# Query and key rows copied from SBUF into the score stacks, and a new order of the lead-in of a two-layer attention and mixture kernel

## The chip, the cores and the metric

One core of a Trainium2 chip runs the whole program. The metric is the device time of one execution in microseconds. TensorE is called PE below, VectorE DVE, ScalarE ACT, GpSimd POOL and SyncE SP; "SPq" and so on is an engine's sequencer, which issues DMAs.

## The reference, cut to what matters

The input is x (4 batches, 512 tokens, 256 channels) and a context of the same shape. Two layers follow each other:

```
x = x + xattn0(layernorm(x), ctx)      # 16 heads of 16 channels, biases, score bias -0.1*|i-j|
x = x + ffn0(layernorm(x))             # dense SiLU MLP + product-key retrieval: top 8 of 1024 experts, 4 heads
x = x + xattn1(layernorm(x), ctx)      # 16 heads, relu on q, k and v, no biases
x = x + ffn1(layernorm(x))             # 8 experts, top 2 by a gate, gelu MLP 256-512-256
```

Each attention is softmax(q k^T / 4 [+ bias]) v for every batch and head. What matters here is how q and k get to the place where PE multiplies them.

## The kernel before, in words

Everything is fp32, and where a product must be exact to more bits than one pass gives, a value is held as a rounded high part and the rest (low part). For attention, each head's q and k are laid in *stacks*: `sq` and `sk` hold, for each of 8 pairs of heads, 64 partitions per head of the pair (`HALF`), of which 48 (`BROW`) are three blocks of 16 rows (q: high, low, high; k: high, high, low), then 8 rows of constants (the bias by distance), then the row of maxima (`MROW`). One product over 56 or 57 partitions so gives the exact score with its bias.

A batch is prepared by *jobs*: "xt" (transposes of the normed x), "k" and "q" (projections, two of each, `i` or `s` = 0, 1 being the first or second head of each pair), "v" (values), later "on"/"wo" (output projection). For "k" and "q" ACT writes the high part into the row buffer `hl` and DVE the low part (L1593, L1594); `hl` is [128, 4, 2, 512]: index 0 and 1 are queries, 2 and 3 keys. `write_rows` (SP) then writes each to a DRAM tensor `qk_rows` by two DMAs (L468, L469), and after all eight of a batch have landed (`s_dw`), `load_stacks` and `stack` (L482) read them back in the stacks' layout, four DMAs of 192 KB for each of four head groups `g`.

An attention layer runs in steps U = -7 to 63 and a few more, 16 steps to a batch, four to a head group. Step U does the four score products for the row maxima of group (U+7)/4 (L1161; DVE reduces each, L1589; three PSUM banks), the scores by key of its own (L1175), their exponential (ACT, L905), in layer 0 a factor for near keys (POOL, L670), and the values (L1194). The table of jobs is written out by hand: `PREPARE` and `PREPARE_SECOND` (for batch 1) give the step of each job relative to its batch's step 0, `FINISH` those of the output projection, `STACKS` the steps at which SP loads the stacks, `NEXT_CTX` those of the next context. `FIRST` is the order of batch 0's jobs, ahead of the steps.

Each engine works through its own queue in order. Before the steps of layer 0: SP issues the loads of x and context of batch 0, all constants and weights, then waits for the rounded row patterns (`s_rowc`), spreads them into the stacks (`const_rows`, L493, L496: 9 or 8 partitions each), writes key rows, loads x of batches 1 to 3 and reads its half of the stacks. ACT loads wk, wq, wv, empties PSUM, writes the query rows (`first_query_rows`, L916, L917) and reads the other half (`first_stacks`, L925). DVE computes the statistics of batch 0, waits for all query weights and scales them (L1816), normalises (`first_norm`, L1667), and in its `prologue` (L1782 to L1808) turns the products of the retrieval weights (`wret`), the gate's constants and the output bias out of PSUM and computes the statistics of batches 1 to 3 at once. PE's `prologue` (L1220 to L1235) computes these products. POOL adds the output bias to x (`add_bo`) and norms the later batches (`norm`, L620); in the steps of layer 0 it also splits layer 1's expert weights into high and low parts by way of DRAM (`split_high`, `split_low`, `split_out` L655, `load_raw` L660, L661).

Layer 1's first rows are prepared at the end of ffn0; `first_rows` (SP) writes and reads them.

## Time and profile before

| | us |
|---|---|
| median of 3 runs | 1217.73 (1215.11 to 1217.9) |
| profiled execution | 1213.62 |
| its span | 1211.8 |
| PE busy | 1055.4 (87%) |
| DVE busy | 788.4 (65%) |
| ACT busy | 638.7 (53%) |
| POOL busy | 474.4 (39%) |

In the profile's rows, `L1161` is a line of the kernel, `out<-in` names the tensors, `xN` counts instructions merged into a row, and what stands in brackets with `<-` is the idle time before an instruction and what ended it. Rows of the timeline begin with start and duration in us. A DMA-issuing row (SPq, ACTq, POOL DMA_DIRECT2D) is the time that the sequencer takes to issue, not the transfer.

### The profile page before, as it was taken

To read this page: it belongs to the slowest core of one execution; us is meant where nothing else is said; L and a number is where in the kernel's file an instruction comes from. 1 tells how busy PE (TensorE), PEld (TensorE's weight loads), DVE (VectorE), ACT (ScalarE), POOL (GpSimd) and SP (SyncE) were. 2 spreads that over 40 slices of the span, in tenths; PEclk is the share of its full clock that TensorE was granted. 3 is DMA by queue.
4 is the path that set the end of the run, shared out by engine and by line. 5 is a ranking of instruction groups with operands and counts; after the bars stand their busy time and mean duration, and the time that the engine had idled before them with its cause. 6 is when DMAs were issued, how large, how long until landed. Compare 5 with 4: busy or idle time off the path is not lost.

```text
span 1211.8 us, 16920 instructions
## 1 busy us (share of the span) xinstructions
PE 1055.4 (87%) x5478; PEld 658.8 (54%) x5478; DVE 788.4 (65%) x1986; ACT 638.7 (53%) x848; POOL 474.4 (39%) x494
## 2 busy tenths in 40 slices
PE   9499899989776999999999778999999888799991
PEld 5134343434355787787777554433334334588881
DVE  3667677786489777877787334777777955244443
ACT  2146565566528667667677422565545661355550
POOL 1347777686413243343443321212323334222220
PEclk9579999999879999999999986999998998899996
DMA  7946778666999300000002330455453328222226
GB/s 186 249 148 192 228 198 264 174 206 224 255 238 233 78 1 1 1 1 1 1 1 64 103 78 1 148 165 146 117 167 93 102 63 325 66 74 71 72 62 209
DMA packets 75595, 151.71 MB, mean 125 GB/s; under 512 B 8234, under 2 KB 45356, under 8 KB 73974
## 3 DMA queue, kind: packets, MB, share of 16 engines
q1 hardware_dynamic: 62518, 99.46, 31.9%
q0 software_dynamic: 10544, 47.23, 11.2%
q10 hardware_dynamic: 2448, 3.94, 1.2%
q8 instruction: 47, 0.77, 0.3%
q14 instruction: 38, 0.31, 0.1%
HBM read 73.88 MB, written 76.25 MB: 124 GB/s over the span
## 4 chain that ended last, share of the span: by engine, by line
PE 55%; DVE 24%; ACT 8%; issue 6%; POOL 3%; DMA 3%; SPq 1%; ACTq 0%; DVEq 0%; POOLq 0%
PE ps L1296 14%; DVE negmax L1589 9%; PE ps L1194 7%; PE ps L1161 6%; PE ps L1140 4%; PE ps L1175 4%; PE ps L1149 4%; PE ps L1398 3%; PE ps L1375 3%; PE ps L1361 2%; PE ps L1203 1%; PE ps L1516 1%; DVE moe_w L1885 1%; DVE hl L1594 1%; DVE on L1609 1%
## 5 line engine op out<-in xcount | busy, mean ns | idle before, releaser
L1589 DVE TENSOR_REDUCE negmax<-ps 128x1 f32<-128x512 f32 x512 | 320.9, 682 | 68.9 <-PE ps L1161 67.2
L905 ACT ACTIVATE pt<-ps 128x1024 f32<-128x1024 f32 x256 | 256.4, 1026 | 129.9 <-PE ps L1175 129.1
L1161 PE MATMUL ps<-sk,sq 56*128 56x512 f32 x512 | 166.5, 460 | 48.0 <-DVE negmax L1589 24.7
L1194 PE MATMUL ps<-pt,v_aug 128*32 128x512 f32 x1024 | 142.6, 620 | 1.2 <-POOL pt L670 0.8
L1161 PEld LDWEIGHTS ps<-sk,sq 56*128 56x128 f32 x512 | 75.7, 200 | 105.3 <-DVE negmax L1589 76.3
L1175 PE MATMUL ps<-sq,sk 57*128 57x512 f32 x512 | 127.1, 489 | 2.5 <-DVE negmax L1589 1.4
L670 POOL TENSOR_TENSOR pt<-pt,near 128x256 f32<-128x256 f32 x128 | 92.3, 728 | 76.0 <-ACT pt L905 75.7
L1175 PEld LDWEIGHTS ps<-sq,sk 57*128 57x128 f32 x512 | 50.1, 190 | 101.2 <-issue 72.4
L835 POOL DMA_INDIRECT expert_out<-yo,dest x39 | 38.2, 980 | 116.2 <-ACT yo L1080 104.5
L751 POOL TENSOR_TENSOR w_first<-w_first,moe_w 128x1024 f32<-128x1024 f32 x16 | 38.1, 2379 | 105.7 <-DVE pt L1877 105.0
L1361 PE MATMUL ps<-sel,hl 128*128 128x512 f32 x256 | 71.7, 412 | 5.6 <-DVE pt L1877 5.6
L1296 PE MATMUL ps<-wexp,ghl 128*128 x468 | 65.9, 290 | 1.6 <-DVE ghl L1985 1.5
L1296 PE MATMUL ps<-wexp,xhl 128*128 x234 | 65.0, 414 | 1.2 <-DVE xhl L1981 1.2
L1985 DVE TENSOR_TENSOR ghl<-ps,ghl 128x512 fp32r<-128x512 f32 x39 | 26.9, 691 | 59.8 <-ACT ghl L1073 59.8
L1375 PE MATMUL ps<-wup_e,xn 128*128 128x256 f32 x256 | 62.1, 379 | 0.0
L1296 PEld LDWEIGHTS ps<-wexp,ghl 128*128 128x128 f32 x468 | 57.9, 188 | 6.4 <-issue 2.2
L806 POOL TENSOR_TENSOR x_tok<-x_tok,on 128x256 f32<-128x256 f32 x16 | 11.6, 725 | 121.7 <-DVE on L1609 121.7
L1877 DVE SCALAR_TENSOR_TENSOR moe_w<-ps,thr,moe_w 128x1024 f32<-128x1024 f32 x26 | 33.3, 1280 | 39.7 <-ACT moe_w L966 39.6
L1361 PEld LDWEIGHTS ps<-sel,hl 128*128 128x128 f32 x256 | 48.0, 188 | 16.3 <-DVE pt L1877 6.9
L966 ACT ACTIVATE moe_w<-ps,negm 128x1024 f32<-128x1024 f32 x26 | 28.9, 1112 | 52.2 <-PE ps L1361 30.3
L1375 PEld LDWEIGHTS ps<-wup_e,xn 128*128 128x128 f32 x256 | 48.1, 190 | 7.8 <-issue 1.0
L797 POOL DMA_INDIRECT expert_rows<-pay,rowi x32 | 31.8, 994 | 44.1 <-DVEq L1751 35.9
(284 smaller groups left out, 2008.2 us busy)
## 6 DMA issues: line engine op xcount, KB each, us to landing
expert_rows<-zero SPq DMA_DIRECT2D x3, 5586.0 KB, 58.0
expert_weights_split<-wst POOLq DMA_DIRECT2D x8, 2048.0 KB, 9.4
qk_rows<-hl SPq DMA_DIRECT2D x30, 512.0 KB
sq<-qk_rows SPq DMA_DIRECT2D x60, 192.0 KB, 4.6
sk<-qk_rows SPq DMA_DIRECT2D x60, 192.0 KB, 5.1
moe_w<-in_w POOLq DMA_DIRECT2D x16, 512.0 KB, 7.1
wexp<-expert_weights_split POOLq DMA_DIRECT2D x16, 512.0 KB, 4.6
wexp<-expert_weights_split SPq DMA_DIRECT2D x4, 2048.0 KB, 17.1
```

Of the source, the lines that this page charges most:

```text
L670: pool.tensor_tensor(probs, probs, near[:].unsqueeze(1).broadcast_to([P, 2, P]), ALU.mult).then_inc(s_near, 1)
L835: pool.indirect_dma_start(yg, bass.IndirectOffsetOnAxis(ap=dest[:, j:j + 1], axis=0), yo[:, j % 3, :], None, bounds_check=2 * NTOK - 1, oo ...
L905: act.activation(pt[:, 4 * (U % 2) + 2 * half:4 * (U % 2) + 2 * half + 2, :], ps[:, 2 + 2 * half:4 + 2 * half, :], ACT.Exp, scale=(BIAS, S ...
L1140: ins = pe.matmul(dst, w[L][:, part, i * P:(i + 1) * P], src[:, part, :], start=(part == 0), stop=(part == 1))
L1149: ins = pe.matmul(dst[:, part * D:(part + 1) * D], src[:, k, t * P:(t + 1) * P], w[:, k, :], start=(k == 0), stop=(k == KC - 1))
L1161: pe.matmul(ps[:, jbank(job), :], sq[r, pair, t * P:(t + 1) * P], sk[r, pair, :], start=True, stop=True).then_inc(s_job, 1)
L1175: ins = pe.matmul(ps[:, 2 + 2 * half + s, :], sk[r, pair, c * P:(c + 1) * P], sq[r, pair, :], start=True, stop=True)
L1194: ins = pe.matmul(ps[32 * j:32 * j + 32, OBANK, :], v_aug[:, b % 2, c, HG * g + j, :], pt[:, 4 * (U % 2) + j, :], start=(c == 0), stop=(c ...
L1296: ins = pe.matmul(dst, lhs(i), rhs(j), start=(first and i == j == 0), stop=(last and i == 1))
L1361: ins = pe.matmul(dst[:, j, :], turned[n % 2][:, i, h * P:(h + 1) * P], sel[:, NX * YK * j:NX * YK * (j + 1)], start=(i == 0), stop=(i == 1))
L1375: ins = pe.matmul(ps[:, YBANK, (n % 2) * D:(n % 2 + 1) * D], accT[:, c * P:(c + 1) * P], wup_e[:, c, :], start=False, stop=True, skip_grou ...
L1589: dve.tensor_reduce(negmax[:, n % 2, col:col + 1], src, AX, ALU.max, negate=True).then_inc(s_jd, 1)
```

## The change

The DRAM tensor `qk_rows`, `write_rows` and `s_dw` go. The order of the projections' columns is changed (last lines of the diff), so that the rows of one head group are 32 neighbouring partitions of `hl`; `stack` copies them straight into the stacks, three DMAs of 64 KB for each half and each of `sq` and `sk`, twelve for a group, 48 for a batch. ACT's write of the next batch's rows into `hl` now waits for the last group's copies (`s_ld[3]`). `PREPARE`, `STACKS`, `NEXT_CTX` and `FINISH` get new steps. In `first_rows` the two halves are copied one after the other.

In the lead-in SP loads x and context of batches 0 and 1, copies the key stacks, then the selector and the rest. POOL issues `const_rows` of layer 0 and the eight loads of weights. DVE rounds the row patterns and norms batch 0 before it waits for the query weights; its `prologue` goes: POOL scales the gate's columns (`gate_columns`), ACT copies the products out of PSUM, POOL takes the low parts (`wret_low`) and adds the bias (`bias_out`); the statistics of batches 1, 2, 3 go to DVE's steps -3, 0, 1, and the inverse deviations of 2 and 3 are computed by Newton steps on POOL. PE's `prologue` keeps the retrieval products; those of gate and bias follow step -4 (`gate_prologue`). ACT issues group 0's query copies ahead of emptying the value jobs, the others behind. The diff, cut:

```diff
-PREPARE = {-22: ("xt", 0), -21: ("xt", 1), -20: ("k", 0), -17: ("k", 1), -16: ("q", 0), -15: ("q", 1), -13: ("v", 0), -12: ("v", 1)}
-PREPARE_SECOND = {-17: ("xt", 0), -16: ("xt", 1), -15: ("k", 0), -14: ("k", 1), -13: ("q", 0), -12: ("q", 1), -11: ("v", 0), -10: ("v", 1)}
-FINISH = {21: ("on", 0), 22: ("on", 1), 23: ("wo", 0), 24: ("wo", 1)}
+PREPARE = {-17: ("xt", 0), -16: ("xt", 1), -14: ("k", 0), -13: ("k", 1), -12: ("q", 0), -11: ("q", 1), -10: ("v", 0), -9: ("v", 1)}
+PREPARE_1 = {-16: ("k", 0), -15: ("k", 1), -14: ("xt", 0), -13: ("xt", 1), -12: ("q", 0), -11: ("q", 1), -10: ("v", 0), -9: ("v", 1)}
+prepared = lambda L, b: PREPARE_1 if L == 0 and b == 1 else PREPARE
+STACKS = {-10: 0, -8: 1, -4: 2, 0: 3}
+FINISH = {22: ("on", 0), 23: ("on", 1), 24: ("wo", 0), 25: ("wo", 1)}
...
-STEPS = (range(-LEAD, LASTU + 9), range(-LEAD, LASTU + 18))
-prepared = lambda b: PREPARE_SECOND if b == 1 else PREPARE
-STACKS = (None, 10, 12, 12)
-NEXT_CTX = (-LEAD, -9)
+STEPS = (range(-LEAD, LASTU + 10), range(-LEAD, LASTU + 18))
+NEXT_CTX = (2, -8)
...
-        rows = nc.dram_tensor("qk_rows", (2, B, 4, 3, P, T), F32, kind="Internal").ap()
...
+            def stack(g, s, dst):
+                for i, part in enumerate((0, 1, 0) if dst is sq else (0, 0, 1)):
+                    at_row = HALF * s + DH * i
+                    sp.dma_start(dst[at_row:at_row + DH, 2 * g:2 * g + 2, :].bitcast(F32),
+                                 hl[2 * DH * g:2 * DH * (g + 1), s if dst is sq else 2 + s, part].bitcast(F32)).then_inc(s_ld[g], 16)
...
+                sp.wait_ge(s_st, 2 * (LASTU * L + NU * (b - 1) + 4 * g + 3) + 2)
                 for s in range(2):
-                    stack(L, b, g, s, sq)
-                    stack(L, b, g, s, sk)
-            def stack(L, b, g, s, dst):
-                src = rows[L, b, s if dst is sq else 2 + s].rearrange("l (i e) t -> (l i) e t", e=NPAIR)
-                sp.dma_start(dst[HALF * s:HALF * s + BROW, 2 * g:2 * g + 2, :].bitcast(F32), src[:, 2 * g:2 * g + 2, :]).then_inc(s_ld[g], 16)
+                    if g == 0:
+                        sp.wait_ge(s_jd, at[L, "k", b, s].done)
+                    stack(g, s, sk)
+                for s in range(2):
+                    if g == 0:
+                        sp.wait_ge(s_jd, at[L, "q", b, s].done)
+                    stack(g, s, sq)
...
                 sp.wait_ge(s_hd, NTL)
                 for s in range(2):
-                    const_rows(1, s, sk)
-                for g in range(NG):
-                    for s in range(2):
-                        stack(1, 0, g, s, sk)
+                    const_rows(sp, 1, s, sk)
                 for s in range(2):
-                    write_rows(1, 0, "q", s)
+                    sp.wait_ge(s_pre, 1 + s)
+                    for g in range(NG):
+                        stack(g, s, sk)
                 sp.wait_ge(s_f, NTL)
                 sp.wait_ge(s_zr, 1)
                 for s in range(2):
-                    const_rows(1, s, sq)
-                sp.wait_ge(s_dw, 128 * (B + 1))
-                for g in range(NG):
-                    for s in range(2):
-                        stack(1, 0, g, s, sq)
+                    const_rows(sp, 1, s, sq)
+                for s in range(2):
+                    sp.wait_ge(s_pre, 3 + s)
+                    for g in range(NG):
+                        stack(g, s, sq)
...
+            sp.dma_start(st_rows, a["c_rows"]).then_inc(s_rows_in, 16)
+            sp.wait_ge(s_wk, 16 * 2)
+            sp.dma_start(x_tok[:, 1], tokens(a["x"][1])).then_inc(s_x[1], 16)
+            load_ctx(0, 1)
+            for g in range(NG):
+                for s in range(2):
+                    if g == 0:
+                        sp.wait_ge(s_jd, at[0, "k", 0, s].done)
+                    stack(g, s, sk)
+            sp.dma_start(st_sel, a["c_sel"]).then_inc(s_selin, 16)
+            for b in range(2, B):
+                sp.dma_start(x_tok[:, b], tokens(a["x"][b])).then_inc(s_x[b], 16)
             for dst, src in ((tab[:], a["c_tab"]), (before16[:], a["c_before"])):
                 sp.dma_start(dst, src).then_inc(s_tab, 16)
-            sp.wait_ge(s_rowc, 1)
...
+            pool.wait_ge(s_rowc, 1)
+            for s in range(2):
+                const_rows(pool, 0, s, sk)
+                const_rows(pool, 0, s, sq)
+            for dst, src in (
+                (st_wq, a["w_ret"].rearrange("(a n) d -> n a d", n=RD)), (st_keys, a["keys"].rearrange("n h p k -> n (h p k)")),
+                (bo_bc[:], a["bo"].rearrange("(a n) -> a n", a=1).broadcast_to([P, D])), (bvc[:], a["bv"]),
+                (gw[:, :, 0:ME], kcut(a["gate"])), (gcol[:, 0:KC], a["gamma"]),
+                (gcol[:, KC:2 * KC], a["beta"]), (wo[:], kcut(a["wo0"])),
+            ):
+                pool.dma_start(dst, src).then_inc(s_w, 16)
+            own = Own(pool, s_pown)
...
+            def wret_low(k):
+                pool.wait_ge(s_wret, 2 * k + 2)
+                pool.tensor_tensor(wret[:, 1, k, :], wret_full[:, k, :], wret[:, 0, k, :].bitcast(F32), ALU.subtract).then_inc(s_wrl, 1)
+            def bias_out():
+                pool.wait_ge(s_wret, 2 * KC + 3)
+                pool.tensor_tensor(bo_bc[:], bo_full, bo_bc[:], ALU.add).then_inc(s_bo_bc, 1)
...
-                if U in (2, 3):
-                    norm(0, 2, range(2 * U - 4, 2 * U - 2))
-                if U == 4:
-                    add_bo(2)
-                if U in (14, 21):
-                    norm(0, 3, range(0, 2) if U == 14 else range(2, 4))
-                if U == 26:
-                    add_bo(3)
+                if U == 2:
+                    add_bo(0)
+                if U in (3, 4):
+                    rstd_newton(range(0, 2) if U == 3 else range(2, NEWTON))
+                if U in (4, 8):
+                    wret_low((U - 4) // 4)
+                if U in (9, 14):
+                    norm(0, 2, range(0, 2) if U == 9 else range(2, 4))
+                if U in (21, 26):
+                    norm(0, 3, range(0, 2) if U == 21 else range(2, 4))
+                if U == 33:
+                    add_bo(1)
+                if U in (45, 46):
+                    add_bo(U - 43)
...
-                        act.wait_ge(s_dw, 128 * (B * L + job.b))
+                        act.wait_ge(s_ld[NG - 1], 192 * (B * L + job.b))
...
+                    if job.kind == "v" and job.i == 0:
+                        first_stacks(0)
...
-                    for s in range(2):
-                        first_query_rows(s)
-                    for g in range(NG):
+                    for g in range(1, NG):
                         first_stacks(g)
+                    for k in range(KC):
+                        act.wait_ge(s_wret_ps, k + 1)
+                        act.copy(wret[:, 0, k, :], ps[:, 2 + k, :]).then_inc(s_wret, 1)
+                        act.copy(wret_full[:, k, :], ps[:, 2 + k, :]).then_inc(s_wret, 1)
+                    act.wait_ge(s_wret_ps, KC + 1)
+                    act.copy(bo_full, ps[:, OBANK, 0:D]).then_inc(s_wret, 1)
+                    for i in range(2):
+                        act.copy(gbc[:, i, :], ps[:, 4 + i, 0:ME]).then_inc(s_wret, 1)
+                    sqrt(1, sd[:, 1, :], mv[:, 1, :, 1])
+                    act.wait_ge(s_selin, 16)
+                    act.copy(sel[:], st_sel).then_inc(s_sel, 1)
+                    act.wait_ge(s_ci, 16 * NCI)
                     act.activation(near[:], st_dist, ACT.Exp, scale=-BIAS).then_inc(s_nr, 1)
-                    sqrt(1, sd[:, 1:B, :], mv[:, 1:B, :, 1])
                 for U in STEPS[L]:
                     Ug = LASTU * L + U
...
+                for s in range(2):
+                    if g == 0:
+                        act.wait_ge(s_jd, at[0, "q", 0, s].done)
+                    for i, part in enumerate((0, 1, 0)):
+                        at_row = HALF * s + DH * i
+                        act.dma_start(sq[at_row:at_row + DH, 2 * g:2 * g + 2, :].bitcast(F32), hl[2 * DH * g:2 * DH * (g + 1), s, part].bitcast(F32)).then_inc(s_ld[g], 16)
...
-                    pe.wait_ge(s_ld[v // 4], 64 * (B * L + job.b + 1))
+                    pe.wait_ge(s_ld[v // 4], 192 * (B * L + job.b + 1))
...
+                    if L == 0 and U == 0:
...
+                    if L == 0 and U == -4:
+                        gate_prologue()
...
+                    if L == 0 and U == -3:
+                        batch_stats(1)
+                        dve.sem_inc(s_lnv, 1)
+                    if L == 0 and U == -2:
+                        dve.wait_ge(s_lnd, 2)
+                        dve.reciprocal(rstd[:, 1, :], sd[:, 1, :]).then_inc(s_rstd, 1)
+                    if L == 0 and U in (0, 1):
+                        batch_stats(2 + U)
+                    if L == 0 and U == 2:
+                        flat_bt = lambda v: v.rearrange("p b t -> p (b t)")
+                        root_seed(flat_bt(rstd[:, 2:B, :]), flat_bt(mv[:, 2:B, :, 1]), root[:, 0, 0:2 * TT]).then_inc(s_lns, 1)
...
-            dve.wait_ge(s_wqk, 16 * 3)
-            dve.tensor_scalar(wq[0][:], wq[0][:], SCALE * UNITS, None, ALU.mult).then_inc(s_conv, 1)
+            dve.wait_ge(s_rows_in, 16)
+            dve.tensor_copy(rowc[:], st_rows).then_inc(s_rowc, 1)
             dve.wait_ge(s_lnd, 1)
             dve.reciprocal(rstd[:, 0, :], sd[:, 0, :]).then_inc(s_rstd, 1)
             first_norm()
+            dve.wait_ge(s_wqk, 16 * 3)
+            dve.tensor_scalar(wq[0][:], wq[0][:], SCALE * UNITS, None, ALU.mult).then_inc(s_conv, 1)
             dve.tensor_scalar(bqk[:, 0, :], bqk[:, 0, :], SCALE * UNITS, None, ALU.mult).then_inc(s_conv, 1)
-            dve.wait_ge(s_ci, 16 * NCI)
-            dve.tensor_copy(rowc[:], st_rows).then_inc(s_rowc, 1)
             attention(0)
...
-    order = np.array([(2 * e + s) * DH + ch for s in range(2) for ch in range(DH) for e in range(NPAIR)])
+    order = np.array([(2 * e + s) * DH + ch for s in range(2) for g in range(NG) for ch in range(DH) for e in (2 * g, 2 * g + 1)])
...
```

## Rows read from the trace of the kernel before

**Rows 1.** The page: busy us, share and instructions of each engine

```profile
PE 1055.4 (87%) x5478; PEld 658.8 (54%) x5478; DVE 788.4 (65%) x1986; ACT 638.7 (53%) x848; POOL 474.4 (39%) x494
```

**Rows 2.** The chain of waits, 0 to 130 us: start, duration, what

```profile
3.40 7.67 DMA w_first<-in_wv
...
30.56 16.81 issue
...
48.19 11.45 DVE negmax L1589 x19
...
70.34 3.72 PE ps L1140 x4
...
82.14 2.00 PE ps L1140 x4
```

**Rows 3.** The timeline of the lead-in and first steps: start, duration, engine, line, operation

```profile
11.64 1.38 DVE L1667 TENSOR_SCALAR xn<-x_tok,mv,rstd 128x256 f32<-128x256 f32 x4
...
22.08 0.75 DVE L1594 SCALAR_TENSOR_TENSOR hl<-ps,bqk,hl 128x512 fp32r<-128x512 f32 x1 [1.37 <-ACT hl L871]
...
24.64 3.78 PE L1225 MATMUL ps<-moe_w 64*128 64x64 f32 x32
...
29.26 1.30 PE L1234 MATMUL ps<-w_first,pt 128*128 128x256 f32 x4
...
39.36 1.41 DVE L1554 BATCH_NORM_STATS2 st<-x_tok 128x6 f32<-128x256 f32 x4
...
41.26 0.45 ACTq L925 DMA_DIRECT2D sk<-qk_rows  x1
...
47.38 1.19 PE L1161 MATMUL ps<-sk,sq 56*128 56x512 f32 x3 [16.81 <-issue]
...
64.81 0.65 PE L1175 MATMUL ps<-sq,sk 57*128 57x512 f32 x2
...
71.11 0.82 POOL L661 DMA_DIRECT2D moe_w<-in_w  x1
```

**Rows 4.** Windows: us, busy time by engine, PE's clock, DMA share, GB/s

```profile
core 0: us, PE busy (x) PEld busy (x) DVE busy (x) ACT busy (x) POOL busy (x), PEclk, DMA share, GB/s
14.00:22.00 8.00, 6.74 (x17) 3.44 (x18) 1.75 (x3) 2.00 (x4) 0.00 (x0) 0.79 0.44 58
28.00:38.00 10.00, 2.56 (x16) 1.85 (x15) 3.04 (x8) 0.00 (x0) 2.33 (x1) 0.60 1.04 353
...
697.00:699.00 2.00, 0.27 (x2) 0.00 (x0) 0.00 (x0) 2.00 (x3) 2.00 (x2) 1.00 0.46 49
704.00:708.00 4.00, 3.11 (x15) 2.11 (x13) 1.48 (x3) 0.11 (x1) 2.15 (x1) 1.00 1.03 214
```

**Rows 5.** The line L482 (stack DMAs), 160 to 215 us: time to landing

```profile
DMA to landing us min/median/max: 3.3/4.8/6.2
```

**Rows 6.** The timeline of layer 0's steps, several engines

```profile
98.74 0.42 SPq L482 DMA_DIRECT2D sk<-qk_rows  x1
...
123.89 0.50 PE L1161 MATMUL ps<-sk,sq 56*128 56x512 f32 x2 [2.06 <-DMA sk<-qk_rows]
...
131.41 2.43 POOL L620 TENSOR_SCALAR xn<-x_tok,mv,rstd 128x256 f32<-128x256 f32 x2
...
134.58 0.51 PE L1175 MATMUL ps<-sq,sk 57*128 57x512 f32 x2
...
137.04 0.62 POOL L655 DMA_DIRECT2D expert_weights_split<-wst  x1
...
146.12 0.50 PE L1175 MATMUL ps<-sq,sk 57*128 57x512 f32 x2
```

**Rows 7.** The timeline where layer 1's scores start

```profile
695.14 1.47 SPq L496 DMA_DIRECT2D sq<-rowz  x2
...
706.38 0.73 PE L1161 MATMUL ps<-sk,sq 56*128 56x512 f32 x3
...
709.08 4.84 DVE L1589 TENSOR_REDUCE negmax<-ps 128x1 f32<-128x512 f32 x8
```

182 lines of the change are left out of this document (66 added, 116 removed).

## The prediction

> **What bounds the kernel now.** I read the page first: PE is busy 87% of the span [rows 1], so what it does not do must be looked for in few places. Then the chain of waits in order of time: its one hole in the first 130 us is 16.81 us of "issue" before the first score product at 47.38, after which DVE's row maxima (11.45 us for 19) carry the chain, then PE [rows 2]. The timeline shows what fills the hole: the last query rows are complete in SBUF at 22.8 (22.08 + 0.75), they are written to DRAM and read back into the stacks, the last reading DMA is issued at 41.3, and PE starts at 47.38; step 0 starts at 64.81 [rows 3]. The windows show the DMA engines full from 28 to 38 at 353 GB/s, and PE's granted clock falling there to 0.60 on average [rows 4]. From step 0 to the end of layer 0 PE has almost no gaps, so there the change can gain little and can lose. So three places count: the lead-in, the handover of the row buffer hl from batch to batch, and the start of layer 1's scores.
>
> **Lead-in, first part: until the query rows are complete.** The first norm starts at 11.64 since its reciprocal stands in DVE's queue behind the wait for all query weights, which land at 11.07 [rows 2, 3]. With the norm first it starts once the deviations are there, a good 1.5 us earlier; PE's transposes follow its own key products, so I carry 1.5 us through: rows complete at 21.3.
>
> **Second part: rows to stacks.** Removed are four times 768 KB of writes, the wait for all of them, and as much reading. Added are 48 DMAs of 64 KB, each to 16 partitions, in place of 16 of 192 KB to 48. The 24 key ones are issued by SP from about 12.4 on, at 0.42 us each [rows 6] by 23; of the query ones ACT issues the six of group 0 by about 23, ahead of emptying the value products. How fast such a copy goes no row shows. Lower bound: DMAs to 8 partitions moved 49 GB/s from 697 to 699 [rows 4]; upper: those to 48 partitions 214 GB/s from 704 to 708 [rows 4]. Twice eight partitions would be 98 GB/s, 0.67 us each; at the issue rate it is 0.42 us, 150 GB/s. I take 150, since successive copies go to other partitions and may overlap, and keep 98 for the range. The first groups then land by 26.
>
> The Trainium skill speaks against the change here: "SBUF — State Buffer", section "Door 1: The DMA port swizzle", says that a DMA's rate goes by the ports that its partitions reach, and gives 104 GB/s for partitions 0 to 15. The 49 and 214 GB/s of this trace agree with it as far as they go; by it every group would take an estimated 7.6 us in place of 5.2, which is the second rival below.
>
> **Third part: the constants.** PE's products of the retrieval weights (3.78 us for 32) [rows 3] stand ahead of the first score and wait for all eight loads that now leave by POOL. POOL can start once the row patterns are rounded (about 9, my estimate: it follows batch 0's statistics on DVE), issues 12 DMAs at 0.82 us each [rows 3] until 19, and the first four are the slow kind: 544 KB at 58 GB/s, as from 14 to 22 now [rows 4], is 9.4 us. The 1.1 MB of weights behind them share the DMA engines with the stacks: 3 us if alone at 353 GB/s, 7 at 155. I take 27 for their landing; +3.8 us of products gives the first score at 31 (bounds 27.5 and 38), against 47.38: **-16.4 us**. The work that hid these products until now was the round trip, which is gone; hence they count whole.
>
> **Fourth part: steps -7 to -1.** They take 17.4 us now (47.38 to 64.81) at DVE's pace. DVE gets statistics of one batch (1.41 us [rows 3] and 0.4 for the aggregates) and waits for ACT's square root, which needs a table load; PE gets the gate's and bias's products (1.30 us for four of them) [rows 3] while DVE has at most three banks to work on: **+2.5** (1.8 to 5). ACT's 18 further stack DMAs, some 8 us of its sequencer, and its copies of wret lie beside DVE's maxima; without that cover (98 GB/s and a full ring) they push the root back by up to 3 us. The selector and x of batches 2 and 3 stand behind 24 stack DMAs on SP and land by 45 to 55, where ACT and DVE ask for them.
>
> **Steps 0 to 7.** A key product now falls in step 0, where the clock is still low: four parts took 3.72 us there against 2.00 at full clock [rows 2]. Two more statistics (1.8 us each) go on DVE beside a PE that is busy. One pair of transposes leaves DVE-bound steps: **+1.5** (0 to 3).
>
> **Layer 0 after that.** Gone is the 2.06 us stall on a key stack in step 13 [rows 6], since group 1 is asked for two steps earlier: **-2**. POOL's second half of batch 2's norm (2.43 us) stood in step 14 for batch 3 and ended at 133.8 [rows 6]; it is now wanted by PE's step 15 at once, about 132.5: **+1.3**. New is the wait of ACT: before it writes the next batch's key rows into hl, all 48 DMAs of the last batch must have landed (they leave from hl itself). The last twelve leave after the second half of step 15; the next key job is in step 18. From 134.58 to 146.12 [rows 6] it is 11.5 us; with transposes and nothing where two query products stood (-3.3) and with the key product itself (+2.6) it is 10.9. Twelve DMAs need 0.9 + 5.2 + 2 = 8 us alone, 11 at 98 GB/s, and a write of 2 MB starts in the middle of it at 137.04 [rows 6]. Behind ACT's wait stand that step's second exponential and with it PE. The landing of four DMAs now takes 3.3 to 6.2 us under the same load [rows 5]. I take +1 us for each of two handovers, **+2** (0 to 10).
>
> **Layer 1.** The query stacks' constants leave at 695.14 [rows 7] and move at 49 GB/s until 701; behind them come all of half 0, then half 1, so group 0 is whole with the 15th DMA: 701 + 15 x 0.42 + 1.5 = 709, or 712.5 at 98 GB/s. The first score is at 706.38, but DVE takes it up only at 709.08 [rows 7], so **+1** (0 to 4). Two handovers with less other traffic: **+0.6** (0 to 4). The tail is untouched.
>
> **Sum.** -16.4 + 2.5 + 1.5 - 2 + 1.3 + 2 + 1 + 0.6 = -9.5. The profiled execution took 1213.62 us (span 1211.8) and becomes 1204.1; the median of the three runs lies 4.1 above the profiled one, so 1217.73 becomes **1208.2**. What the unknown costs span by themselves: -16 to +3.
>
> **The rivals.** *Hidden throughout*: the copies keep the issue rate, no handover waits, first score at 28: 13 to 15 us less than now, 1203. For it: hl is read at SBUF's side alone and DRAM traffic falls by 24 MB each way. *The narrow copies run at 98 GB/s*: each batch then holds the DMA engines some 32 us; the first score slips to 35 (+4 against my sum), handovers in layer 0 cost 3 each (+4), layer 1's start 4 (+3), the rest 1: 1220 less some overlap, I put it at 1218. For it: the 49 GB/s row, with ends as far as 8 and 48 partitions only; against it, that successive copies alternate between partitions. *POOL's queue is the new bound of the lead-in*: slow constants, then weights behind full rings, weights in at 34, first score at 38; 7 of the 16 us go: 1215. The lead-in would then not be much shorter, whatever the stacks do. *Slower*: the handover of hl. One mechanism: ACT's wait for the last twelve copies. It decides once they land later than 10.9 us after their start; with the 2 MB write and 1 MB of raw weights between them that can be 17 us, and then each of four handovers costs 6 where I took 1 or less: +21 against my sum, with part of it hidden 1226.
>
> **How the numbers follow.** My forecast (1204 to 1213) 0.50; hidden throughout 0.12; narrow copies 0.18; POOL's queue 0.09; slower 0.11. 0.3% is 3.7 us, about what a measurement of this kernel can tell from no change: faster is below 1214, slower above 1221.4. Faster: 0.50 + 0.12 + a third of the POOL case and of the narrow one's low end, 0.70; same 0.18; slower 0.12. The range leaves out the slower case and the best of the hidden one: 1201 to 1221.
>
> **What would show it.** Right: first score product near 31, behind the retrieval products and those behind POOL's loads; step 0 near 51; no gap before the key products of steps 18 and 34; in windows the stack copies above 140 GB/s. Wrong: ACT waiting on stack DMAs before a key row; copies near 100 GB/s with full DMA engines; PE idle on query stacks at 706 to 712; PE's retrieval products later than 30.

## The result, and the profile of the changed kernel

The changed kernel takes 1242.2 us (median of 4 runs, 1238.2 to 1244.7) against 1216.8 before (4 runs on the same chip): a ratio of 1.021, 95% interval 1.017 to 1.024. It is 25 us slower, not 9.5 faster. Its profiled execution took 1238.23 us (span 1236.4), 24.6 more than the one of before, which is the difference that the steps below divide up. Runs of a kernel that lie over 1.5% above its fastest are left out of every comparison here; that is so for two runs of max_act alone.

The page of the changed kernel: PE is busy 8.5 us longer and the span is 24.6 us longer [rows 1]. In the chain of waits (second line) DMA now has 6% and SP's issuing 4%; before it was 3% and 1%.

```profile
PE 1063.9 (86%) x5478; PEld 666.5 (54%) x5478; DVE 787.3 (64%) x1976; ACT 639.7 (52%) x854; POOL 488.9 (40%) x526
...
PE 52%; DVE 22%; ACT 7%; DMA 6%; issue 5%; SPq 4%; POOL 3%; DVEq 0%; POOLq 0%; ACTq 0%
```

The timeline of its lead-in (L1266 the retrieval products, L1202 the score products for the maxima, L1277 the output bias, L1216 the scores by key, whose first is step 0):

```profile
32.47 6.66 PE L1266 MATMUL ps<-moe_w 64*128 64x64 f32 x30 [11.59 <-DMA w_first<-in_wo]
38.72 0.79 PE L1202 MATMUL ps<-sk,sq 56*128 56x512 f32 x1
...
50.49 2.05 PE L1277 MATMUL ps<-w_first,pt 128*128 128x256 f32 x4
...
61.15 1.12 PE L1216 MATMUL ps<-sq,sk 57*128 57x512 f32 x2
```

The first score product starts at 38.72 against 47.38, but step 0 at 61.15 against 64.81 [rows 3]: of 8.7 us, 3.7 are left. PE waits 11.6 us for the last of the weights that POOL loads (`in_wo`, issued at 16.89 and landed at 32.4), at the end of which its clock is at half, so that the products take 6.66 us and not 3.78.

The timeline of the steps: SP's queue (L473 stack copies, L467 context, L491 maxima), where the maxima stand ready (L1646), POOL's write of 2 MB (L688), and what waits:

```profile
94.81 3.79 SPq L473 DMA_DIRECT2D sk<-hl  x6
...
106.25 4.60 SPq L473 DMA_DIRECT2D sq<-hl  x6
108.00 0.61 POOL L688 DMA_DIRECT2D expert_weights_split<-wst  x1
108.47 0.28 DVE L1646 CAST m_sb<-ps 16x128 fp32r<-16x128 f32 x1
110.89 1.71 SPq L467 DMA_DIRECT2D ctxT<-in_ctx  x1
112.64 2.79 SPq L491 DMA_DIRECT2D sq<-m_sb  x2
...
122.93 0.79 PE L1216 MATMUL ps<-sq,sk 57*128 57x512 f32 x2 [7.96 <-DMA sq<-m_sb]
...
144.13 6.36 SPq L473 DMA_DIRECT2D sq<-hl  x6
...
156.48 0.69 ACT L907 ACTIVATE hl<-ps,bqk 128x512 fp32r<-128x512 f32 x1 [7.72 <-DMA sq<-hl]
...
158.07 1.12 PE L1244 MATMUL ps<-ident,oT 128*128 128x128 f32 x4 [6.63 <-DVE hl L1640]
...
160.27 3.78 PE L1181 MATMUL ps<-ctxT,w_first 128*128 128x512 f32 x4
```

Two stalls stand here that before did not have. In step 12 PE waits 8.0 us for the row of maxima, whose DMAs SP issued behind 24 copies and a context load: the row was ready at 108.75, its DMAs were issued from 112.64 on, and PE could start at 122.93, 14.2 us after the row was ready. Part of the way is the DMA engines' load, since POOL's 2 MB write stands beside it; but the kernel before has the same write at 107.99 and no such wait. (A copy issued at 106.9 landed 2.3 us after its issue began, one issued at 109.4, behind the write, 8.4 us.) In step 18 ACT waits 7.7 us for the last copies to leave `hl`, and PE 6.6 us with it. The windows show what each leaves behind: PE's clock at 0.54 of full after the first, and a key product of 3.78 us in place of 1.98 after the second.

```profile
core 0: us, PE busy (x) PEld busy (x) DVE busy (x) ACT busy (x) POOL busy (x), PEclk, DMA share, GB/s
...
120.00:135.00 15.00, 11.82 (x45) 4.83 (x49) 6.57 (x12) 6.15 (x7) 8.12 (x7) 0.54 0.36 85
```

Layer 1's first score waits 4.7 us for query copies (timeline, SP and PE):

```profile
721.85 13.22 SPq L473 DMA_DIRECT2D sq<-hl  x16
736.36 1.19 PE L1202 MATMUL ps<-sk,sq 56*128 56x512 f32 x3 [4.74 <-DMA sq<-hl]
```

A second way to read the traces, which works since all these kernels make the same products in the same order of steps: for each step, the start of its first score by key, minus the start of the same product in the kernel before (a positive number is time lost up to there). All later tables of this kind are read from the profiled executions; "score" is the first score product, "step 0" its key product, both in us from the start. Jobs stand in other steps in the change, so at steps 11 to 19 the two have not done the same work; at 0, 7, 26, 46 and 61 they nearly have.

```
                score  step 0 |  0     7    13    19    26    46    61 | layer 1: 2    62
before           47.4    64.8
changed kernel   38.7    61.2 | -3.7  -2.6   6.2   9.2  17.4  24.4  24.4     25.9  24.8
```

So: 8.7 us gained ahead of the first score, 5.0 given back by step 0, 1.1 by step 7, 27 by the end of layer 0, 3.7 at layer 1's start (where DVE takes up the first score), and 3.5 regained behind it.

### The profile page after: what moved, and what is told of

Same layout as the page of the kernel before. It is cut to its first block, busy times and chain, and to the rows that moved or that the text cites. A ratio compares the mean times of both kernels' runs of the same rounds, so it can differ in the third digit from the quotient of the medians.

```text
span 1236.4 us, 17126 instructions
## 1 busy us (share of the span) xinstructions
PE 1063.9 (86%) x5478; PEld 666.5 (54%) x5478; DVE 787.3 (64%) x1976; ACT 639.7 (52%) x854; POOL 488.9 (40%) x526
## 3 DMA queue, kind: packets, MB, share of 16 engines
q0 software_dynamic: 11312, 48.85, 12.5%
## 4 chain that ended last, share of the span: by engine, by line
PE 52%; DVE 22%; ACT 7%; DMA 6%; issue 5%; SPq 4%; POOL 3%; DVEq 0%; POOLq 0%; ACTq 0%
PE ps L1341 14%; DVE negmax L1635 8%; PE ps L1235 6%; PE ps L1202 6%; PE ps L1216 4%; PE ps L1181 4%; SPq L473 3%; PE ps L1443 3%; PE ps L1190 2%; PE ps L1406 2%; PE ps L1420 2%; DMA sq<-m_sb 2%; PE ps L1562 1%; DMA sq<-hl 1%; DMA w_first<-in_wo 1%
## 5 line engine op out<-in xcount | busy, mean ns | idle before, releaser
L1202 PE MATMUL ps<-sk,sq 56*128 56x512 f32 x512 | 171.4, 472 | 34.7 <-DVE negmax L1635 25.7
L1235 PE MATMUL ps<-pt,v_aug 128*32 128x512 f32 x1024 | 146.2, 634 | 1.1 <-POOL pt L703 0.8
L1216 PE MATMUL ps<-sq,sk 57*128 57x512 f32 x512 | 129.0, 501 | 13.6 <-DMA sq<-m_sb 11.5
L1202 PEld LDWEIGHTS ps<-sk,sq 56*128 56x128 f32 x512 | 79.0, 206 | 93.9 <-DVE negmax L1635 79.6
L1216 PEld LDWEIGHTS ps<-sq,sk 57*128 57x128 f32 x512 | 51.3, 197 | 113.6 <-issue 64.9
L655 POOL TENSOR_SCALAR xn<-x_tok,mv,rstd 128x256 f32<-128x256 f32 x24 | 29.3, 1225 | 58.9 <-PE ps L1420 33.4
L842 POOL TENSOR_TENSOR x_tok<-x_tok,on 128x256 f32<-128x256 f32 x16 | 11.7, 731 | 94.9 <-DVE on L1655 94.8
```

Source lines behind the costliest of these rows:

```text
L1202: pe.matmul(ps[:, jbank(job), :], sq[r, pair, t * P:(t + 1) * P], sk[r, pair, :], start=True, stop=True).then_inc(s_job, 1)
L1216: ins = pe.matmul(ps[:, 2 + 2 * half + s, :], sk[r, pair, c * P:(c + 1) * P], sq[r, pair, :], start=True, stop=True)
L1235: ins = pe.matmul(ps[32 * j:32 * j + 32, OBANK, :], v_aug[:, b % 2, c, HG * g + j, :], pt[:, 4 * (U % 2) + j, :], start=(c == 0), stop=(c ...
```

## The experiments

Times are medians with the ratio to runs of the kernel before on the same chip. Single runs of one kernel lie up to 10 us apart, some more; the long ones show a lower mean clock (rows_only 1245.0 us at 0.919, 1262.8 at 0.899). Where a stage is in question the verdict rests on the step table, not on the time.

### The two stalls, one by one

**Maxima issued by ACT.** The edit, in ACT's loop behind its first exponential of the step, with the same two DMAs:

```diff
-                        if u + 2 in (0, 4, 8, 12):
-                            load_max(L, b, (u + 2) // 4)          # SP
+                            if U % 4 == 2 and 0 <= U + 2 < LASTU:
+                                load_max(L, (U + 2) // NU, (U + 2) % NU // 4)   # ACT
```

> The changed kernel, but the two DMAs of the row maxima of each head group are issued by ACT in place of SP, where they stand behind the stack copies. Theory (the maxima wait in SP's queue): the stalls of 8.0, 1.6 and 1.9 us before the key products of steps 12, 32 and 48 are gone, and with them the low clock behind them (0.54 from 120 to 135); 12 to 15 us less than the changed kernel's 1242.2, so 1227 to 1230. Rival (the DMA engines are full with the copies and loads of that stretch, 258 GB/s, whoever issues): the maxima still land 5 us or more after their issue, the stall in step 12 stays above 4 us; time 1236 to 1242.

Its times, 1233.9 and 1241.3 beside two near 1256, give no verdict. The timeline has the stall of 8.0 us down to 2.75, with the DMAs issued at 112.15 and landed by 120.9:

```profile
112.15 2.39 ACTq L956 DMA_DIRECT2D sq<-m_sb  x2
...
120.89 0.79 PE L1216 MATMUL ps<-sq,sk 57*128 57x512 f32 x2 [2.75 <-DMA sq<-m_sb]
```

So both readings hold in part. From the ready row (here at 111.91) to PE's start it is 9.0 us in place of 14.2: the queue order made 5.2 of the 8.0 us, but even from a queue of their own two DMAs of 4 KB took over 6 us, with the DMA engines 92% busy from 111 to 121. The key product of step 12 came only 2.0 us earlier, since in this run PE had reached it 3.2 us later; and the low clock behind the stall did not go with it (0.50 over 120 to 135, where the changed kernel has 0.54). Over layer 0 the waits for maxima add up to 12.5 us in five places, no less than the 11.5 in three before the edit (8.0, 1.6 and 1.9 us, in steps 12, 32 and 44; the expectation has 48 for the last).

**Key and query rows handed over apart.**

```diff
-                        act.wait_ge(s_ld[NG - 1], 192 * (B * L + job.b))
+                        act.wait_ge(s_kld if which else s_ld[NG - 1], 96 * (B * L + job.b))
```

> The changed kernel, but ACT's write of a batch's key rows waits for the last group's six key copies alone (their own semaphore), its write of the query rows for the six query copies. Theory (the handover of hl): the key copies of batch 1's last group are issued by 144.1 and land by 148, before ACT comes to the key rows in step 18; the wait of 7.7 us there is gone, one of 0 to 3 us may stand before the query rows two steps later; with the low clock behind it (a key product of 3.78 us in place of 1.98) 7 to 10 us less, 1232 to 1235. Rival (the key copies too land late, behind the 2 MB write at 141.16): the wait shrinks by less than 3 us; time 1239 to 1242.

1241.2 us (1.020, 1.013 to 1.026). The wait in step 18 is 1.16 us in place of 7.72:

```profile
151.63 0.69 ACT L908 ACTIVATE hl<-ps,bqk 128x512 fp32r<-128x512 f32 x1 [1.16 <-DMA sk<-hl]
```

The mechanism is as expected (step 26 at +10.6 in place of +17.4), but the time is not: by layer 0's end it stands at +22.4. The waits for the maxima are those of the changed kernel (11.7 us in three places); what takes 4.8 us more than there between steps 26 and 61 is the clock. The windows over these steps (key_wait first, then the changed kernel) hold the same 690 products, which take PE 5.1 us longer at a mean clock of 0.93 in place of 0.96:

```profile
189.00:331.00 142.00, 131.09 (x690) 54.67 (x690) 100.26 (x194) 81.92 (x95) 101.73 (x109) 0.93 0.55 175
196.00:333.00 137.00, 126.00 (x690) 53.04 (x688) 100.05 (x193) 82.02 (x95) 101.27 (x109) 0.96 0.57 182
```

**Both.** The two edits together.

> The changed kernel with both: row maxima issued by ACT, and key and query rows of hl handed over apart. Theory (the two waits are separate and each had hidden nothing of the other): key products of step 12 start near 121, of step 18 near 146 and of step 26 near 181 to 184, against 122.9, 147.1 and 195.8; layer 0's attention ends 10 to 16 us earlier than in the changed kernel; time 1226 to 1232. Rival (the copies' load on the DMA engines, or the jobs' new steps, take the time elsewhere once the two stalls are gone): step 26 near 190 or later, time 1236 to 1242.

1245.5 us (1.022, 1.018 to 1.025): the rival's time, though up to step 26 nearly the theory's steps (118.9, 145.7 and 185.1 us for steps 12, 18 and 26).

```
                score  step 0 |  0     7    13    19    26    46    61 | layer 1: 2    62
max_act          39.9    62.4 | -2.4   0.6   4.1   8.9  16.7  23.3  32.3     32.2  27.9
key_wait         38.3    60.7 | -4.1  -1.7   6.6   3.9  10.6  20.0  22.4     20.8  26.4
bc               38.7    61.1 | -3.7  -1.3   1.9   0.7   6.7  15.8  28.2     28.1  33.9
bc_gated         38.9    61.3 | -3.5   0.1   3.5   0.9   7.0  13.7  19.1     19.3  25.1
```

Step 26 is at +6.7, 10.7 us better than the changed kernel. Then it loses 21 us. Part of it shows in SP's queue and at PE:

```profile
289.34 32.57 SPq L540 DMA_DIRECT2D expert_rows<-zero  x2
...
331.20 1.22 PE L1219 MATMUL ps<-sq,sk 57*128 57x512 f32 x4 [5.31 <-DMA sq<-m_sb]
```

SP's wait for the last maxima had held back what follows in its queue, a zero fill (four DMAs of 5586 KB; the expectation below counts three), until 326; without that wait it starts at 289, over the last three groups. In max_act it starts at 295, with a stall of 4.8 us at the same place.

**The fill held back.** As bc, with one wait in SP's queue ahead of layer 1's loads:

```diff
             attention(0)
+            sp.wait_ge(s_jd, at[0, "m", B - 1, NG - 1].done)
             load_ctx(1, 0)
```

> As bc, but SP waits for the last row maxima of layer 0 before it goes on to layer 1's contexts and the zero fill of the experts' rows (16.8 MB), as it did when it issued the maxima itself. Theory (in bc SP, free of the maxima, began the fill at 289 us and not at 327, beside the last copies, POOL's weight loads and three batches of maxima, whose DMAs then came late: a wait of 5.3 us at 331): the waits behind step 48 fall below 2 us each, layer 0's attention ends 6 to 9 us earlier than in bc; time 1236 to 1240. Rival (the waits come from the copies themselves): they stay, time 1243 to 1247.

1235.0 us (1.015, 1.010 to 1.019), a little better than the theory has it, and the stall near the end of layer 0 is gone (+19.1 in place of +28.2 at step 61). Four waits for maxima, 8.4 us together, stay in its layer 0; what makes them was not taken apart.

### The lead-in

**Retrieval products behind step -5.**

```diff
-                if L == 0:
-                    prologue()
...
+                    if L == 0 and U == -5:
+                        prologue()
```

> The changed kernel, but PE's 32 products of the retrieval weights stand behind step -5, between DVE-bound score products, in place of ahead of the first score. Theory (POOL's late weights, complete at 32.4 us, and the 6.66 us of cold products behind them hold the first score): it comes at 31 to 33 in place of 38.7, step 0 at 55 to 57; time 1236 to 1238. Rival (the group 0 copies, issued by ACT from 17.5 to 25.2 with the DMA engines full, land no earlier than 36): first score at 36 or later, time 1240 to 1242.

1248.3 us (1.025, 1.018 to 1.031): neither. The first score comes 3.4 us earlier, step 0 1.9 us later (63.1). The products, at half clock, stand between score products that DVE waits for: it is idle for 5.9 us over them. (More PSUM banks ahead of them might have hidden them; that was not run.) The first score product is not what counts, step 0 is.

**Weights ahead of the row patterns.** POOL's eight loads moved above its wait for `s_rowc`.

> The changed kernel, but POOL issues the eight loads of weights ahead of its wait for the row patterns and not behind the four spreading DMAs. Theory (the weights, complete at 32.4 us, hold PE's retrieval products and with them all that follows): products at 21 to 26 at full clock, first score product at 29 to 33, step 0 at 51 to 55 in place of 61.2; the steps as in the changed kernel; time 1233 to 1237. Rival (the group 0 copies or DVE's and ACT's queues hold steps -7 to -1, as the run retr_later hints, where the first score came 3.4 us earlier and step 0 1.9 us later): step 0 at 58 or later, time 1239 or more.

1236.2 us (1.018, 1.013 to 1.022).

```profile
21.41 3.78 PE L1266 MATMUL ps<-moe_w 64*128 64x64 f32 x32
30.67 1.19 PE L1202 MATMUL ps<-sk,sq 56*128 56x512 f32 x3 [5.48 <-issue]
```

The first score is at 30.7 and step 0 at 52.5, 8.7 us earlier than in the changed kernel. The late weights cost that much, and it was the order of POOL's queue alone. That the prediction had 31 for the first score is luck: it had PE's products end there, and here they end at 25.2 and PE then waits 5.5 us for the last of group 0's copies, which lands at 30.6.

**All four.**

> The changed kernel with the maxima by ACT, the handover of hl by halves, the gated fill and the weights first. Theory (the four causes add up): step 0 at 51 to 55, step 26 at 175 to 180, layer 0's attention ends 15 to 20 us earlier than in the changed kernel; time 1220 to 1228, still slower than the kernel before at 1217, since the copies go on costing in the steps. Rival (each wait removed comes back as another one): time 1234 or more.

1229.4 us (1.011, 1.007 to 1.014): 12.7 us better than the changed kernel, and still slower than before, a little outside what the theory gave. Steps 0 to 61 still cost 18.5 us against before (-11.7 to +6.8), where the changed kernel's cost 28.1. With the weights the causes named so far explain half of the loss, but only a third of what the steps lose; so the halves of the change were taken apart next.

```
                score  step 0 |   0     7    13    19    26    46    61 | layer 1: 2    62
retr_later       35.3    63.1 |  -1.7   0.1   9.4  11.9  19.3  28.1  30.2     30.5  36.5
weights_first    30.7    52.5 | -12.3  -9.0  -0.9   0.5   8.3  15.2  15.4     17.7  19.7
all_fixes        31.3    53.1 | -11.7  -6.5  -3.5  -6.3  -0.3   4.0   6.8     10.3  16.1
```

### The change taken apart

**Old lead-in, rows straight into the stacks, new steps of the jobs.**

> The kernel before with the rows copied straight into the stacks and the changed kernel's steps of the jobs, but the old order of the lead-in: constants and weights by SP, DVE's prologue, statistics ahead of the steps. Theory (the two halves are separate; the steps lose 25 to 29 us by the copies, the lead-in gains by the round trip that is gone): first score product at 31 to 35, since the weights land early as before, step 0 near 50 to 54; the stalls in steps 12 and 18 and the end of layer 0's attention as in the changed kernel less some 8 us; time 1228 to 1236. Rival (the new order of the lead-in gave what the lead-in gained): first score at 38 or later, time 1240 or more.

1248.9 us (1.029, 1.022 to 1.036). First score at 34.1, then step 0 at 71.2. DVE's row tells why; its statistics waited for x, which SP loaded behind 24 copies:

```profile
49.58 1.41 DVE L1528 BATCH_NORM_STATS2 st<-x_tok 128x6 f32<-128x256 f32 x4 [18.26 <-DMA x_tok<-in_x]
```

**The same with x loaded ahead of the row patterns.**

> As the run rows_only (rows straight into the stacks, the changed kernel's steps, the old order of the lead-in), but x of batches 1 to 3 and the second context are loaded ahead of the row patterns and key copies, so that DVE's statistics of these batches lie in its idle time. Theory (in rows_only the statistics waited for x behind 24 key copies until 49.6 us, which alone made step 0 late at 71.2): first score product at 31 to 35, step 0 at 50 to 54; from there the steps lose by the copies as in the changed kernel, so that layer 0's attention ends 12 to 17 us later than before; time 1229 to 1235. Rival (the key and query copies at 150 GB/s would hold the later groups, and steps -7 to -1 take over 22 us all the same): step 0 at 57 or later, time 1235 or more.

1243.4 us (1.022, 1.017 to 1.026): step 0 at 62.2 only, the rival's case. Both stalls are there (8.4 and 5.9 us). What holds step 0 back is found in the next two runs.

**Old lead-in and old steps; only batch 0 straight into the stacks.** Later batches go through DRAM, group by group.

> The kernel before, old lead-in and old steps, but batch 0's rows go straight into the stacks, and x of batches 1 to 3 is loaded as in rows_x_early; later batches by way of DRAM, group by group (writes cut in four by group, reads of 192 KB). Theory (the copies pay where PE waits for the round trip, and cost where they are hidden): first score product at 31 to 35 in place of 47.4, step 0 at 50 to 54 in place of 64.8, steps as before; 8 to 14 us less than before: 1204 to 1210. Rival (the first stretch is bound elsewhere, by DMA time or PE's low clock): step 0 at 58 or later, or the gain is gone by step 12; time 1213 to 1218.

1213.7 us (0.999, 0.997 to 1.001): no difference that can be told. The steps are those of before within 1.3 us from 0 to the end of layer 1. This and the run before it have nearly the same lead-in up to step 0 (62.2 and 63.5), so **the copies in the steps, with the places of the jobs that they force, cost 29.7 us** (1243.4 less 1213.7, uncertain by some 6 us by the two intervals). POOL's norms and bias additions for later batches move with them. The jobs must move since the copies leave from `hl` itself, and `hl` is free only when the stacks of the last batch are.

The lead-in gained nothing although the first score came 10.7 us earlier. ACT's timeline names the cause (L927 query copies, L931 the root that DVE's reciprocals wait for, ahead of its first maximum at 46.9):

```profile
32.40 11.04 ACTq L927 DMA_DIRECT2D sq<-hl  x16
...
46.40 0.30 ACT L931 ACTIVATE sd<-mv,eps 128x12 f32<-128x12 f32 x1
```

**The reciprocals behind step -4.**

```diff
-                dve.wait_ge(s_lnd, 2)
-                dve.reciprocal(rstd[:, 1:B, :], sd[:, 1:B, :]).then_inc(s_rstd, 1)   # prologue
+                    if L == 0 and U == -4:
+                        dve.wait_ge(s_lnd, 2)
+                        dve.reciprocal(rstd[:, 1:B, :], sd[:, 1:B, :]).then_inc(s_rstd, 1)
```

> As before_direct0, but DVE takes the reciprocals of the deviations of batches 1 to 3 behind its maxima of step -4, in place of ahead of the first maximum. Theory (in before_direct0 DVE held its maxima until 46.9 us for ACT's root, which stood behind 18 query copies of 0.6 us issue each, so that the first score at 36.7 gained nothing): maxima from 37.5 on, step 0 at 53 to 56 in place of 63.5, and nothing given back later; 7 to 10 us less than before_direct0: 1204 to 1208. Rival (PE's half clock and three PSUM banks, or batch 1's norm, bind the stretch): step 0 at 60 or later, time 1210 to 1214.

**1204.7 us (0.990, 0.988 to 0.992): faster than both kernels.** The maxima start at 37.7, step 0 at 54.4, and the steps give 2.4 of the 10.4 us back, the rest stays to the end. (Moving the reciprocals in the kernel before was not run; its trace has them at 44.99, ahead of its first score product at 47.38, so there they hold nothing up.)

```profile
37.68 9.65 DVE L1591 TENSOR_REDUCE negmax<-ps 128x1 f32<-128x512 f32 x16 [0.26 <-DVE mv L1561]
47.26 0.21 DVE L1639 RECIPROCAL rstd<-sd 128x12 f32<-128x12 f32 x1
```

**The same with batch 0's norm first.**

> As direct0_root, but DVE norms batch 0 before it waits for the query weights, as in the change. Theory: the norm starts 1.5 to 2 us earlier, the query rows are complete as much earlier, first score product at 33.5 to 34; but DVE's statistics of three batches, which end at 37.5, stand ahead of the first maximum and hide most of it: 0 to 1.5 us less than direct0_root, 1203 to 1205. Rival (all of it is carried through): 1202 to 1203.

1207.8 us (0.993, 0.991 to 0.996), nothing gained, as neither reading had it. The query rows are complete at 19.9 and the first score still comes at 36.4: the last of group 0's twelve copies lands at 36.3, so the copies bound it, not the rows.

**The same with the change's places for the value and output jobs.**

> As direct0_root (later batches by way of DRAM), but with the places that the change gives to the value and output jobs: v in steps -10, -9 of its batch and on, wo in 22 to 25, so that two steps of a batch hold a v and an on job at once and fewer steps hold one. Theory (the copies cost in the steps, the places of the jobs little): layer 0's attention ends within 3 us of direct0_root, the time is 1204 to 1209. Rival (steps without a job are bound by DVE's maxima, and the change has more of them): 2 to 4 us lost for each batch in both layers, time 1212 to 1222.

1209.0 us (0.994, 0.991 to 0.997), 4.3 more than direct0_root; the two intervals overlap a little. In the profile layer 0 loses 8.3 us by it (-8.0 to +0.3 at step 61) and layer 1 nothing. Windows over its steps (PE's clock, the third number from the end, is 1.00 over the same work in direct0_root):

```profile
182.00:222.00 40.00, 37.38 (x178) 13.81 (x174) 27.99 (x52) 23.14 (x27) 27.14 (x29) 0.92 0.90 280
222.00:250.00 28.00, 26.97 (x146) 12.88 (x146) 18.38 (x34) 14.58 (x20) 16.21 (x18) 0.93 0.50 152
```

So 4 to 8 us of the 29.7 are put down to the places of the value and output jobs; some 22 to 26 are left for the copies, and with them the places of the transposes, key and query jobs and of POOL's norms, which no run moved alone. The table shows where each falls: between steps 26 and 46, where all have done nearly the same work, late_jobs loses 5.5 us without a copy in its steps, the changed kernel 7.0 and direct0_root 0.2. Most of what the copies cost lies ahead of step 26, where the changed kernel loses 20.0 us from step 7 on and late_jobs 7.0.

```
                score  step 0 |   0     7    13    19    26    46    61 | layer 1: 2    62
rows_only        34.1    71.2 |   6.4   5.3  13.1  14.9  21.6  30.2  30.1     32.2  31.4
rows_x_early     35.8    62.2 |  -2.6  -2.4   6.8  10.4  17.0  26.9  29.3     27.4  29.9
before_direct0   36.7    63.5 |  -1.3  -1.2  -1.2  -0.4  -0.3   0.1   0.1      0.3  -0.1
direct0_root     35.3    54.4 | -10.4 -10.4 -10.4  -8.2  -8.2  -8.0  -8.0     -9.0  -9.5
direct0_norm     36.4    56.7 |  -8.1  -8.9  -8.9  -6.5  -2.7  -2.7  -2.7      3.8   0.3
late_jobs        35.3    54.0 | -10.8 -12.1 -10.6  -8.3  -5.1   0.4   0.3      1.1  -2.5
order_only       42.8    67.9 |   3.1   6.7  11.6  13.3  13.3  13.4  13.7     19.9  23.1
batch0_direct    39.4    65.5 |   0.7   4.8  11.5   8.2   8.8   8.9   9.2      9.8  13.8
steps_old        38.0    64.0 |  -0.8   2.3  11.4  21.1  36.7  55.6  58.0     60.9 103.0
```

**The new order of the lead-in alone, rows by DRAM.**

> The other half: the changed kernel's order of the lead-in (norm first, constants and weights by POOL, statistics, Newton steps and low parts in the steps), but all rows by way of DRAM and the old steps of the jobs. Theory (the steps lose by the copies alone): first score product at 43 to 48, step 0 at 62 to 66, from there on as in the kernel before, no stall in steps 12 and 18 above 2 us; time 1212 to 1221. Rival (the work moved into the steps costs there): layer 0's attention ends over 6 us later than before although step 0 does not; time above 1223.

1232.6 us (1.011, 1.008 to 1.015): the rival's case. The steps up to 11 lose 8.5 us, later ones 2. Part of that belongs to this run alone: the old steps want batch 2's norm at step 10, and where it was put POOL came late to the near factor (a wait of 2.4 us in step 9). So what the statistics and Newton steps cost by themselves is not settled. The halves do not add either: this run is 15 us slower than the kernel before and rows_x_early 27, the changed kernel with both 25.

**New lead-in, rows of batch 0 direct, the rest by DRAM.** Two forms. In the first a stack is read as 3 blocks times 16 rows, since the new order of the columns parts them:

> The changed kernel's lead-in (batch 0's rows copied in SBUF, loads by POOL, statistics in the steps), but batches 1 to 3 and all of layer 1 by way of DRAM again, with the old steps of the jobs. Theory (what is lost is lost by the copies in the steps): first score product at 38.7 us as in the changed kernel, step 0 near 61, no stall in step 12 or 18 of layer 0, end of layer 0's attention 1 to 4 us earlier than before; time 1212 to 1216 against 1216.8 before. Rival (the statistics, products and norms moved out of the lead-in cost it in the steps): layer 0's attention ends 10 us or more later than before; time above 1225.

1318.6 us (1.085, 1.080 to 1.090): 101 us slower, which neither theory had. In the second the rows lie in DRAM by group, so that the 48 rows are one dimension:

> As the run steps_old, but the rows lie in DRAM group by group, so that a stack's read has 48 rows as its outer dimension again (192 KB each) and not 3 times 16; each write is cut in four by head group. Only batch 0's rows go straight to the stacks. Theory (a DMA whose outer dimension is 3 keeps few of the DMA engines at work, which is what made steps_old slow): the waits for sk<-qk_rows and for the maxima behind them go, layer 0's attention ends within 4 us of the kernel before or earlier; time 1209 to 1218. Rival (the new lead-in or the old steps combined with it cost the time): time above 1250 again.

1226.7 us (1.007, 1.004 to 1.011). The shape of the read, with the writes cut to fit it, was worth 92 us; the rest of its loss is of the size of order_only's and came in the same steps.

### The DMAs by themselves

> Nothing is computed here (x is passed on to the output): stretches of DMAs alone, each behind the end of the last: 24 copies SBUF to SBUF of 64 KB to 16 partitions each as the change makes them, from SP; the same from SP and ACT at once; 8 copies SBUF to SBUF of 192 KB to 48 partitions; 8 reads of 192 KB from DRAM, the 48 rows one outer dimension; the same with the rows as 3 times 16; 24 reads of 64 KB from DRAM to 16 partitions; 6 copies and 6 writes of 256 KB from 128 partitions; single copies. Theory (what costs is the copy from SBUF to SBUF in pieces of 2 KB to 16 partitions): 24 copies in about 15 us by one queue (issue bound, 0.63 us each), 10 us by two at 150 GB/s with full engines, the reads from DRAM above 200 GB/s. Rival 1 (16 partitions are the limit, wherever the data come from): reads of 64 KB from DRAM to 16 partitions are as slow, near 100 to 150 GB/s, and the copy to 48 partitions is faster. Rival 2 (SBUF as source is the limit): the copies to 48 and 128 partitions stay near 150 GB/s too. For the run steps_old: the reads with an outer dimension of 3 take over twice the time of the plain ones.

Windows, each inside one stretch (its columns as above, with POOL alone of the compute engines): copies to 16 partitions from one queue, from two, to 48 partitions, reads of 48 rows, the same as 3 times 16, reads to 16 partitions, copies over 128 partitions. Under them the issue times of the first and of the sixth kind (ns, min/median/max):

```profile
30.00:45.00 15.00, 0.00 (x0) 1.00 0.42 101
48.00:56.00 8.00, 0.00 (x0) 1.00 1.08 138
61.00:68.00 7.00, 0.00 (x0) 1.00 0.97 197
72.00:78.00 6.00, 0.00 (x0) 1.00 0.91 233
82.00:100.00 18.00, 0.00 (x0) 1.00 0.19 77
104.00:114.00 10.00, 0.00 (x0) 1.00 0.52 141
117.00:120.00 3.00, 0.00 (x0) 1.00 1.03 382
L36 SPq DMA_DIRECT2D sk<-hl x43: 560/592/699, 29.2 to 135.0; - x43
L75 SPq DMA_DIRECT2D sk<-qk_rows x24: 332/420/420, 103.0 to 113.5; - x24
```

- One queue of the change's copies moves 101 GB/s with the DMA engines 42% busy: the issue is the bound, 0.59 us each where the same size out of DRAM takes 0.42. Two queues fill the engines (1.08) and reach 138 GB/s. In the windows of rows_only from 32 to 42 us, with little but copies, it is 146 to 153 at 1.08. So neither rival holds alone: a source in SBUF costs issue time, a destination of few partitions costs engine time, since with full engines 16, 48 and 128 partitions give 138, 197 and 382 GB/s.
- The read of 3 times 16 rows keeps 0.19 of the engines busy, which is 3 of 16. That is steps_old.
- A single copy of 64 KB takes 2.3 us from issue to end.

By the Trainium skill, page "DMA: Bandwidth & Descriptors", section "Why a DMA increments its semaphore by 16 and not by 1", a DMA runs on as many of the 16 engines as divide both slowest dimensions: for 3 and 48 that is 3, and the trace agrees (share 0.19, 77 GB/s). By the same rule the maxima's DMAs (2 pairs of one row out of 8) would run on an estimated two engines; no run here shows it. The 104 GB/s of "SBUF — State Buffer", section "Door 1: The DMA port swizzle", is no ceiling for such a series: reads to 16 partitions that alternate went at 141.

## Why the prediction was wrong, by its own steps

**What bounds the kernel.** Right in its places (lead-in, handover, layer 1's start), and incomplete: it named what waits for the rows, and left out the maxima, the other customer of SP's queue.

**Rows complete at 21.3.** They were complete at 19.0. Right, and of no use: here the late weights hold the first score, and where they do not (weights_first, direct0_norm) the copies do.

**The copies.** Issue was taken at 0.42 us from a read out of DRAM [rows 6]; a copy out of SBUF takes 0.59 to 0.63. The rate of 150 GB/s was right for two queues, and the engines are full at it, which the prediction did not draw: a batch's 3 MB then hold them 20 us.

**The constants, first score at 31.** 38.7. Two terms failed: the weights landed at 32.4 and not at 27, and the products behind a wait of 11.6 us ran at half clock (6.66 us, not 3.78). weights_first, where neither happens, has 30.7, though with the copies as the last wait and not the products. This is the rival "POOL's queue", with its first score of 38; it had 0.09.

**Steps -7 to -1, +2.5.** They took 22.4 us against 17.4, +5.0. The gate's and the bias's products were priced from rows at full clock: L1277's four are 2.05 us, not 1.30, and DVE stands idle for 3.5 us meanwhile. The prediction took the low clock into account in step 0 and not here.

**Steps 0 to 7, +1.5.** +1.1. Right.

**Layer 0 after that, -2 + 1.3 + 2.** +27. This is the step that turned the sign, and it failed in three places. (Two of its terms held: the stall on a key stack in step 13 is gone, and the wait for batch 2's norm is 0.67 us.) (1) It gave the copies 0.42 us each on SP and never asked what is queued behind them. At step 10 the maxima stand behind 24 copies and a context load, which is the stall of 8.0 us in step 12; at step 30 behind 12 copies (1.6 us in step 32) and at step 42 behind 24 (1.9 us in step 44). (2) The handover of `hl` was the right mechanism with 1 us where 7.7 were, and in one place of layer 0, not in each: the twelve copies were issued in 11 us beside the 2 MB write, not 5. The "slower" rival had it, with 6 us. (3) The new places of the jobs were priced at nothing but a shift; late_jobs puts 4 to 8 us on them. And the bill is no sum of waits. Of PE's two stalls, 8.0 and 6.6 us, bc takes 12.0 us away and step 26 moves by 10.7; but step 61, in bc_gated, moves by 5.3 only. Its waits for maxima there are 8.4 us against 11.5, and its clock is 0.76 over 262 to 290, where the changed kernel has 0.86 over 272 to 296.

**Layer 1's start, +1.** +3.7: half 0 ahead of half 1 made group 0 wait for its 15th copy, with 4.7 us at PE; inside the bounds of 0 to 4. The handovers there, +0.6, made PE wait nowhere. Layer 1 as a whole, start included, took 0.4 us more than before in this profile, and between 4 less and 9 more in those of the other versions (steps_old aside); that is not explained.

**The rivals.** Three of the four were partly true at once (POOL's queue; narrow copies, as to the full engines and not as to the 98 GB/s with them; the handover), and each was priced as if the others did not occur. None had the maxima.

## What to carry to other kernels

A round trip through DRAM that is hidden costs nothing; replacing it pays only where an engine waits for it. Here that was one batch of eight, and the version that copies directly in that batch alone, with DVE's reciprocals out of the way of its maxima, is the fast one. Before DMAs are added to a queue, list what else is issued from it in the same steps, and give small, late, urgent transfers a queue without bulk ahead of them; then look at what a removed wait had been holding back (here a fill of 22 MB). And follow an earlier start to the next point that all engines must pass: a first product 10 us earlier gained nothing until the engine that uses it was free.
